# The first attention layer of a 16x112x512 decoder: from 128-wide masked scores to 32x32 diagonal blocks turned by VectorE, with one set of layer-norm statistics

## What is computed

```python
def _L0_attn_ref(x, weight_qkv, weight_proj):      # 16 heads of 32, 4 key/value heads
    seq, batch, hidden = x.shape                   # 16, 112, 512: attention runs over the 16
    qkv = (x.reshape(-1, hidden) @ weight_qkv.T).reshape(-1, 4, 192)
    q, k, v = ...                                  # 4 query heads share one key and value head
    scores = jnp.einsum('bhqd,bhkd->bhqk', q, k) * scale
    scores = jnp.where(causal, scores, -inf)       # 16 x 16 for each of the 112 columns of x
    attn = jnp.einsum('bhqk,bhkd->bqhd', softmax(scores), v)
    return attn @ weight_proj.T

x = x + _L0_attn_ref(_layernorm(x), ...)
x = x + _L0_xattn_ref(_layernorm(x), ctx_2048, ...)   # begins with a second layer norm,
                                                      # then divides by 4 scales and rounds to fp8
```

## Time and profile before

| | us |
|---|---|
| median of 3 runs (lowest, highest) | 3667.01 (3666.86, 3668.47) |
| profiled execution | 3677.25 |
| its span, first to last instruction | 3675.5 |
| first layer: first instruction of the loop stage / first maxima of tile 0 / first maxima of tile 13 / last rounding | 26.7 / 40.1 / 291.3 / 342.6 |
| busy in the span | PE 92%, weight loads 73%, DVE 68%, ACT 47%, POOL 26% |

### The profile page before, as it was taken

The page is one execution under the profiler, slowest core; times in us unless marked ns, Lnnn a source line. Parts: engine busy times, 40 slices in busy tenths (PEclk is TensorE's granted clock), DMA queues, the critical chain, the costliest instruction groups (busy, mean ns, idle before and its releaser), DMA issues. The chain is left out here.

```text
span 3675.5 us, 54660 instructions
## 1 busy us (share of the span) xinstructions
PE 3372.4 (92%) x17976; PEld 2700.6 (73%) x17976; DVE 2494.2 (68%) x6490; ACT 1715.9 (47%) x4059; POOL 952.2 (26%) x999
## 2 busy tenths in 40 slices
PE   6884999998799999989999996999989979998999
PEld 4552787787578778777878774888868757776887
DVE  4888889888466666756666666699856555558333
ACT  4653445444343433443443432688627655441222
POOL 2654344444222222332222222200133310000000
PEclk9886999999999999999999997999999989999999
DMA  6113001001100000110000005899930034433000
GB/s 221 21 20 79 0 0 46 23 0 56 44 28 20 19 28 20 55 59 23 20 28 19 20 9 187 290 410 400 353 88 2 12 126 122 124 105 104 11 10 21
DMA packets 113697, 296.12 MB, mean 81 GB/s; under 512 B 38032, under 2 KB 42128, under 8 KB 107776
## 3 DMA queue, kind: packets, MB, share of 16 engines
q1 hardware_dynamic: 107376, 276.39, 21.3%
q0 software_dynamic: 6160, 17.67, 1.6%
HBM read 251.65 MB, written 41.68 MB: 80 GB/s over the span
## 5 line engine op out<-in xcount | busy, mean ns | idle before, releaser
L40 PE MATMUL bank<-w,cross_ctx_part 128*125 128x512 f32 x1536 | 517.2, 418 | 8.1 <-DVE cross_qn L1090 4.7
L40 PEld LDWEIGHTS bank<-w,cross_ctx_part 128*125 128x125 f32 x1536 | 281.8, 187 | 93.5 <-DVE cross_kn L1090 14.5
L1000 ACT ACTIVATE cross_prob<-bank,cross_neg_max 112x375 f32<-112x375 f32 x256 | 147.0, 574 | 359.0 <-DVE cross_neg_max L1096 359.0
L40 PE MATMUL bank<-w_low,cross_ctx_part 128*125 128x512 f32 x768 | 303.7, 395 | 0.0
L1096 DVE TENSOR_REDUCE cross_neg_max<-bank 112x1 f32<-112x375 f32 x256 | 134.0, 524 | 198.0 <-PE bank L872 195.4
L40 PE MATMUL bank<-moe_wt,moe_zT 128*128 128x448 f32 x1176 | 265.1, 374 | 2.1 <-DVE moe_zT L1726 1.5
L1716 DVE TENSOR_TENSOR moe_wt<-moe_raw,moe_wt 128x1792 fp32r<-128x1792 f32 (+1 forms) x111 | 231.6, 2107 | 17.2 <-ACT moe_wt L1614 15.6
L40 PE MATMUL bank<-w,self_xq 128*112 128x512 f32 x512 | 213.7, 417 | 24.1 <-DVE w_low L595 24.0
L40 PEld LDWEIGHTS bank<-moe_wt,moe_zT 128*128 128x128 f32 x1176 | 216.1, 190 | 17.8 <-issue 1.7
L40 PE MATMUL bank<-mlp_zT,mlp_signs 128*128 128x448 f32 x1024 | 220.7, 368 | 5.7 <-DVE mlp_zT L2406 5.7
L772 POOL TENSOR_TENSOR cross_ve<-cross_mv,eps 125x4 f32<-125x4 f32 (+1 forms) x160 | 31.9, 200 | 730.7 <-DVE cross_mv L1081 730.7
(11 more groups left out here) (406 smaller groups left out, 8523.5 us busy)
## 6 DMA issues: line engine op xcount, KB each, us to landing
moe_raw<-in_moe_w SPq DMA_DIRECT2D x74, 896.0 KB, 7.7
moe_raw<-in_moe_w SPq DMA_DIRECT2D x37, 1024.0 KB, 8.2
stream<-in_L1f SPq DMA_DIRECT2D x32, 768.0 KB, 4.2
cross_ctx_raw<-in_ctxT SPq DMA_DIRECT2D x32, 750.0 KB, 4.1
wide_ctxT<-in_ctxT SPq DMA_DIRECT2D x16, 750.0 KB, 4.2
wide_ctx_rows<-in_ctx SPq DMA_DIRECT2D x16, 750.0 KB
expert_rows<-a_zeros SPq DMA_DIRECT2D x1, 8960.0 KB, 26.9
moe_zrow<-expert_rows SPq DMA_DIRECT2D x35, 256.0 KB, 7.8
```

The source lines that it names most:

```text
L40: mm = pe.matmul(out, a, b, start=first and n == 0, stop=last and n == len(pairs) - 1)
L1000: op = act.activation(prob[:, t % SLOTS, i, :], score_bank(t)[0:S, i * NK:(i + 1) * NK], ACT.Exp, bias=neg_max[:, h:h + 1], accum_out=tota ...
```

## The change

- The rows of a tile are ordered by position first (i, b) instead of (b, i), so the 16 rows of a position are neighbours and two positions fill a strip of 32 rows. The host lays `x` out so; the store to `x1` and the copy in `take_z2T` turn the order back.
- `scores` computes only the four 32x32 diagonal blocks of each head. The keys are the stationary operand, so the scores arrive with keys on partitions; strip j of key head r sits in bank r, partitions 32j to 32j+31, with 4 heads x 32 queries as columns. The mask matmuls have 128 columns instead of 512.
- `tops` turns all 128x512 scores out of the four banks with one VectorE transpose of 32x32 blocks (`STREAM_TRANSPOSE`), and takes all 16 maxima per row with one reduction. The exponentials are 32 wide and work in place. `turn_probs` does one reciprocal, one division on DVE (POOL's `divide` is gone) and a second VectorE transpose; `transpose_probs` and `take_probsT` are gone.
- `weigh_values(t)` is now 16 matmuls of 32x32 by 128 columns into banks 0 to 3 and stands one cycle later, after `project_out(t - 1)`; `project_out(t)` stands two cycles after its scores, `transpose_z2(t)` three.
- The statistics of the second norm are derived from those of the first: one `measure`, one power, one `normalise_twice`.
- DVE runs a cycle more: `shift` (with the clipping) and `round_back` of tile t - 4 in cycle t. The mask takes two selections.

The core of the diff; lines that it takes away from the functions printed above are left out where the new ones replace them:

```diff
-        self.ps = [ctx.enter_context(nc.psum_tensor(f"bank{i}", [P, 512], F32)) for i in range(8)]
+        self.banks = ctx.enter_context(nc.psum_tensor("bank", [P, 8, 512], F32))
+        self.ps = [self.banks[:, i, :] for i in range(8)]
...
                                pattern=[[-1, P]], channel_multiplier=1).then_inc(s["masked"], 1)
...
+            pool.affine_select(out=mask[:], in_=mask[:], compare_op=ALU.is_ge, fill=MASKED, base=0,
+                               pattern=[[1, P]], channel_multiplier=-1).then_inc(s["masked"], 1)
+            pool.wait_ge(s["masked"], 2)
+            pool.affine_select(out=mask[:], in_=mask[:], compare_op=ALU.is_ge, fill=MASKED, base=0,
+                               pattern=[[-B, P // B], [0, B]], channel_multiplier=1).then_inc(s["masked"], 1)
...
+            for j in range(4):
+                near = slice(NEAR * j, NEAR * j + NEAR)
+                dve.tensor_copy(mask4[near].rearrange("p (c t) -> p c t", t=NEAR),
+                                mask[near, None, near].to_broadcast([NEAR, 4, NEAR]))
...
+            def root(t):
+                pool.wait_ge(s["vareps"], t + 1)
+                pool.tensor_tensor(rstd[:, t:t + 1], ve[:, t:t + 1], k.half[:, 0:1], ALU.pow).then_inc(s["rooted"], 1)
+            root(0)
+            for t in range(1, NT):
+                root(t)
+                scale_rows(t - 1)
             scale_rows(NT - 1)
...
             def scores(t):
                 pe.wait_ge(s["q_ready"], t + 1)
                 pe.wait_ge(s["k_ready"], t + 1)
...
+                wait(pe, s["out_low"], t - 1)
                 for r in range(4):
...
+                    pe.matmul(ps[r][:, 0:4 * NEAR], ident16[:], mask4[:], start=True, stop=False)
+                for j in range(4):
                     for r in range(4):
...
+                        mm = pe.matmul(ps[r][strip(j), 0:4 * NEAR].rearrange("p (c t) -> p c t", t=NEAR),
+                                       kT[strip(r), strip(j)], qT[strip(r), :, strip(j)], start=False, stop=True)
                 mm.then_inc(s["scores_in_psum"], 1)
             def project_out(t):
                 pe.wait_ge(s["out_low"], t + 1)
+                wait(pe, s["x_done"], t)
                 for c in range(DC):
...
             def weigh_values(t):
...
+                pe.wait_ge(s["probsT_ready"], t + 1)
+                pe.wait_ge(s["scores_turned"], min(t + 2, NT))
+                wait(pe, s["out_low"], t)
                 for r in range(4):
...
+                    for j in range(4):
+                        mm = pe.matmul(ps[j][strip(r), 0:4 * NEAR], kv[strip(j), t % 3, P + 32 * r:P + 32 * r + 32],
+                                       probT[strip(j), t % 2, r].rearrange("p c t -> p (c t)"), start=True, stop=True)
                 mm.then_inc(s["outT_in_psum"], 1)
...
+            for t in range(NT + 3):
+                if t < NT:
+                    scores(t)
                 if t + 1 < NT:
                     project_qkv(t + 1)
+                if 2 <= t < NT + 2:
+                    project_out(t - 2)
+                if 1 <= t < NT + 1:
+                    weigh_values(t - 1)
+                if t + 1 < NT:
                     transpose_q(t + 1)
...
                     transpose_k(t + 1)
...
+                if t >= 3:
+                    transpose_z2(t - 3)
                 if t + 2 < NT:
                     transpose_z(t + 2)
...
+            def exponentials(t):
+                act.wait_ge(s["minus_max"], t + 1)
+                for r in range(4):
+                    for c in range(4):
+                        op = act.activation(prob[:, r, c, :], prob[:, r, c, :], ACT.Exp,
+                                            bias=neg_max[:, r, c:c + 1], accum_out=total[:, r, c:c + 1])
                 op.then_inc(s["exp_done"], 1)
...
+                    op = act.activation(z2T[:, c, :].rearrange("p (b i) -> p b i", b=B),
+                                        tiled(6)[:, c, :].rearrange("p (i b) -> p b i", b=B), ACT.Identity,
+                                        scale=ln_cols[:, c:c + 1], bias=ln_cols[:, DC + c:DC + c + 1])
...
+            for t in range(NT + 3):
+                if t < NT:
+                    exponentials(t)
                 if t + 1 < NT:
                     take_q(t + 1)
...
                     take_kv(t + 1)
...
+                if 1 <= t < NT + 1:
+                    out_high(t - 1)
                 if t + 1 < NT:
                     take_qT(t + 1)
...
                     take_kT(t + 1)
...
+                if t >= 3:
+                    take_z2T(t - 3)
                 if t + 2 < NT:
                     z_high(t + 2)
...
+                if t >= NT:
+                    weights.round_high(act, 0, (QS, KS, VS)[t - NT])
...
             def tops(t):
                 dve.wait_ge(s["scores_in_psum"], t + 1)
...
+                wait(dve, s["probsT_ready"], t)
+                dve.transpose(prob[:].rearrange("p r c t -> p r (c t)"), near_scores).then_inc(s["scores_turned"], 1)
+                dve.wait_ge(s["scores_turned"], t + 1)
+                dve.tensor_reduce(neg_max[:], prob[:], AX.X, ALU.max, negate=True).then_inc(s["minus_max"], 1)
+            def turn_probs(t):
+                dve.wait_ge(s["exp_done"], t + 1)
+                dve.reciprocal(inverse[:], total[:]).then_inc(s["inverse_ready"], 1)
+                dve.wait_ge(s["inverse_ready"], t + 1)
+                dve.tensor_tensor(prob[:], prob[:], inverse[:, :, :, None].to_broadcast([T, 4, 4, NEAR]), ALU.mult)\
+                    .then_inc(s["divided"], 1)
+                dve.wait_ge(s["divided"], t + 1)
+                wait(dve, s["outT_in_psum"], t - 1)
+                dve.transpose(probT[:, t % 2].rearrange("p r c t -> p (r c t)"), prob[:].rearrange("p r c t -> p (r c t)"))\
+                    .then_inc(s["probsT_ready"], 1)
             def out_low(t):
                 dve.wait_ge(s["out_high"], t + 1)
...
+                dve.tensor_tensor(in_strips(oT[1]), heads_of_strips(), in_strips(oT[0]).bitcast(F32), ALU.subtract)\
+                    .then_inc(s["out_low"], 1)
...
+            def measure(t):
                 dve.wait_ge(s["x_done"], t + 1)
...
+                dve.bn_stats(stats[:], xt[:, t, :]).then_inc(s["stat"], 1)
+                dve.wait_ge(s["stat"], t + 1)
+                dve.bn_aggr(mv[:, t, :], stats[:]).then_inc(s["centre"], 1)
+                dve.wait_ge(s["centre"], t + 1)
+                dve.tensor_scalar(ve[:, t:t + 1], mv[:, t, 1:2], 1.0 + EPS, EPS * EPS, ALU.mult, ALU.add)\
+                    .then_inc(s["vareps"], 1)
+            def normalise_twice(t):
+                dve.wait_ge(s["rooted"], t + 1)
                 if t == 0:
                     dve.wait_ge(s["cleared"], 16)
                 wait(dve, s["z2T_in_psum"], t)
...
+                dve.tensor_scalar(z2[:], xt[:, t, :], mv[:, t, 0:1], rstd[:, t:t + 1], ALU.subtract, ALU.mult)\
                     .then_inc(s["z2_ready"], 1)
...
+            def shift(t):
                 dve.wait_ge(s["scaled"], t + 1)
...
+            for t in range(NT + 4):
+                if t < NT:
+                    tops(t)
+                if t >= 4:
+                    shift(t - 4)
+                if 3 <= t < NT + 3:
+                    normalise_twice(t - 3)
                 if t + 2 < NT:
                     normalise(t + 2)
...
+                if t < NT:
+                    turn_probs(t)
+                if 2 <= t < NT + 2:
+                    add_out(t - 2)
+                if 1 <= t < NT + 1:
+                    out_low(t - 1)
+                if 2 <= t < NT + 2:
+                    measure(t - 2)
+                if t >= 4:
+                    round_back(t - 4)
                 if t + 2 < NT:
                     z_low(t + 2)
...
-    lay["x_by_position"] = a["x"].reshape(16, 14, 8, 512).transpose(1, 0, 2, 3).reshape(1792, 512)
+    lay["x_by_position"] = a["x"].reshape(16, 14, 8, 512).transpose(1, 2, 0, 3).reshape(1792, 512)
```

More of the change, by code:

```diff
@@ L2507, in _ @@
         def _(pool):
-            pool.memset(mask[:], MASKED).then_inc(s["made"], 1)
+            pool.memset(mask[:], 0.0).then_inc(s["made"], 1)
             pool.memset(zeros[:], 0.0).then_inc(s["made"], 1)
@@ L2571, in first_layer @@
              "qT_in_psum", "kT_in_psum", "q_ready", "k_ready", "scores_in_psum", "minus_max", "exp_done",
-             "inverse_ready", "probs_ready", "probsT_in_psum", "probsT_ready", "outT_in_psum", "out_high",
-             "out_low", "y_in_psum", "x_done", "cleared", "stat1", "centre1", "vareps1", "rooted1", "z1_ready",
-             "stat2", "centre2", "vareps2", "rooted2", "z2_ready", "z2T_in_psum", "z2T_taken", "scaled", "clipped",
-             "exponent", "magic", "shifted", "rounded")
+             "scores_turned", "inverse_ready", "divided", "probsT_ready", "outT_in_psum", "out_high",
+             "out_low", "y_in_psum", "x_done", "cleared", "stat", "centre", "vareps", "rooted",
```

(17 more changed lines are left out.)

190 lines of the change are left out of this document (25 added, 165 removed).

## The result

| | before | changed |
|---|---|---|
| median of the runs (lowest, highest), us | 3667.74 (3666.86, 3671.02) | 3632.43 (3630.29, 3634.33) |
| profiled execution / its span | 3677.25 / 3675.5 | 3634.33 / 3632.6 |
| first maxima of tile 0 / of tile 13 / end of the last rounding | 40.1 / 291.3 / 342.6 | 37.5 / 249.8 / 308.9 |
| mean cycle, tile 5 to 13 | 20.22 | 18.75 |
| first read of `xq` by the second layer | 343.8 | 310.1 |

The ratio is 0.9902, 95% interval 0.9885 to 0.9919: 35.3 us faster by the medians, against a forecast of 25.4. The loop stage gives 33.7 of it. The two profiled executions differ by 42.9 us; the other 9 lie in the expert layer (1063.4 us before, 1054.4 after, from its first turned tile to the last layer's), which the change doesn't touch.

A forecast was written before the change was run, and what follows sets the result against it. A chain through four engines bounds the loop, with PE waiting for POOL's divisions. Stage terms 38.6 + 62.8 + 136.5 + 18.9 + 16.1 + 44.3 = 317.2 against 342.6 us: 25.4 less, so 3667.0 - 25.4 = 3641.6 us; range 3605 to 3656.

The forecast's parts named there:

- The cycle of 13.95 us: DVE's queue in one full cycle: its instructions sum to 13.95 us if nothing holds it.
- The stop: POOL's scaling enters between two roundings of `round_back`, and DVE stands 3.5 us per cycle, making it 17.5 us.
- The half clock: PE idles 4.9 us for `z_low`, then runs at half clock: 2.0 us lost per cycle, making it 19.5 us.
- the rival at full clock: PE keeps full clock after its wait: cycle 17.5 us, eight cycles by 2.0, 3626 us; chance 0.13.
- Scores and values at 1.2 us each: PE's sixteen 32x32 products of 128 columns cost 1.2 us each for scores and values, priced by today's scores.
- 3634: Time in us if scores and values cost 0.4 us each, values 0.8 us earlier on PE's path in ten cycles.
- The turn: DVE's 32x32 transpose of 512 columns, two added per tile, taken at 0.65 us each.
- The tail: Last cycles, all DVE and POOL: 13.2, 12.6 and 18.5 us, together 44.3 us.
- Slower: PE's 32x32 products don't overlap across strips: sixteen cost 8.4 us, cycle 27.0, 3747 us; chance 0.05.
- The scaling that misses the roundings: POOL's scaling falls beside `z_low` and the maxima instead of `round_back`: cycle 15.6 us at full clock, 3607 us; chance 0.15.
- The dear turn: DVE's 32x32 transpose costs 2.3 us: 1.3 us more in eight cycles, about 2.5 in four, 3662 us; chance 0.06.
- What stood behind the old cycle: Before, DVE's `shift` held up POOL's third and fourth divisions (4.03 us); PE stood 3.12 us and resumed at half clock.

The follow-up runs named there:

- experiment 11: Roundings behind the second normalisation in every cycle, against the kernel with scaling ahead of the power and reordered tail; cycle 14.15 us, next layer at 266.0 us.
- experiment 12: Kernel with scaling ahead of the power and roundings behind the second normalisation in every cycle, timed against before: 3608.08 us, ratio 0.9793.
- experiment 5: Changed kernel with 20 small identity products on PE ahead of its wait for `z_low`, from the sixth cycle on; cycle 16.78 us, next layer at 295.5 us.
- experiment 2: Changed kernel with `round_back` directly behind `shift`; cycle 15.85 us, next layer at 292.2 us.
- experiment 3: Changed kernel with `round_back` directly behind `shift` and POOL's scaling ahead of the power; cycle 14.46 us, next layer at 280.0 us.
- experiment 4: Changed kernel with POOL's scaling in four instructions instead of one; cycle 16.04 us, next layer at 290.5 us.
- experiment 7: Kernel before, with `shift` moved behind `add_out` and the statistics of the rows; cycle 17.51 us, next layer at 319.1 us.

## Where the prediction was right and wrong

**The direction, the size and the mechanism held; one price on the path did not.** The forecast of 3641.6 us was 9.2 too high. The measured 3632.4 lies inside the stated range, but at the very edge of the 3632 to 3655 of the forecast's own case. Of the 8.3 us that the stage gained beyond 25.4, 1.1 lie in the opening (first maxima 37.5, not 38.6), 0.5 in the first five cycles (62.3 against 62.8), 5.4 in the cycles from tile 5 to 13 (150.0 against 155.4), 1.3 in the tail.

- **The cycle of 13.95 us, if nothing holds DVE.** Durations of neighbours overlap by some hundredths in each row; the cycles without any wait, one in experiment 11 and two in experiment 12, took 13.5. In the changed kernel only a part of this error counts, since DVE waits at `add_out` and `out_low` in each full cycle and what is short ahead of them is waited out there. From the start of `out_low` to the next tile's turn the sum has 8.3 us and the rows 8.04: about 2 of the 5.4 us.
- **The stop.** Forecast 3.5 us in each cycle, measured 3.41. That the scaling would fall into `round_back`, and that which rounding it hits does not matter, held: the fourth in the cycle shown, one of the first three in that of experiment 5. The Trainium skill (SBUF — State Buffer, Who interferes with whom) says that a VectorE instruction with two SBUF inputs contends with a GpSimd instruction that reads SBUF, and that their shared ports are an exclusive lock. The rows agree: nothing is lost beside the turn out of the banks and the reduction (0.72 and 0.69 us, experiment 2) and the statistics (0.68, experiment 3), and 0.84 us beside a quarter (experiment 4). One SBUF input alone does not make an instruction safe, as the forecast took it to be. In the kernel before, `normalise`, which writes SBUF from SBUF, takes 1.58 us instead of 0.54 in each of the nine cycles in which the scaling runs beside it (here until 153.76):

```profile
152.47 1.58 DVE L2846 TENSOR_SCALAR a_z<-x,mean_var,rstd 128x512 f32<-128x512 f32 x1
```

- **The half clock.** Forecast 2.0 us lost per cycle, measured 2.0 (18.75 - 16.78). Of the rival at full clock, priced at 16 us, experiment 5 gives 14.6.
- **Scores and values at 1.2 us each, the term that failed.** They take 0.50. I had priced them by products that span all four column groups. The Trainium skill (TensorE: Matmul & The Clock Gate, Measured speedup vs the span model) has the figures from which I had worked out an estimate of 0.4, and that was nearer. For the scores the error was free: `z_low` ends PE's wait, which grew from 4.9 to 5.9. The values are on the path of each full cycle, because DVE waits 0.52 us more behind `add_out` for what ACT takes of them. ACT begins 0.69 us after the values' start (165.21), not 1.2:

```profile
165.90 0.60 ACT L2781 ACTIVATE a_oT<-bank 128x512 fp32r<-128x512 f32 x1 [2.94 <-PE bank L2714]
```

That is 0.5 us in each of eight cycles, about 4 of the 5.4 us; some 0.7 us went back elsewhere. So 3634, the time that the forecast worked out from this estimate, lay nearest to the measured one, and mostly for its own reason, though it counted 0.8 us in ten cycles. The rest of its nearness is luck.
- **The turn** at 0.70 to 0.71 instead of 0.65, **the exponentials** 0.306 apart instead of 0.27: both still hidden or small. The normalisations stay at 0.55.
- **The tail** held to 1.3 us: its roundings read 5.30 for three in cycles 14 to 16, as the earlier trace rows.
- **The rivals.** Slower, by products that don't overlap: refuted by the 0.50 us. The scaling that misses the roundings: not here, but made on purpose in experiment 2, where the cycle was 15.85 for the rival's 15.6. The dear turn: refuted.
- **What stood behind the old cycle.** The reading that `shift` holds up the divisions was right, its weight too low: in experiment 7 moving it takes nearly 3 us off each cycle.

That the 32x32 blocks themselves pay is shown only in the better order: both kernels freed of their stop read 17.51 and 14.15 to 14.46 us per cycle. What part of that belongs to the blocks and what to the single statistics in a cycle that DVE bounds wasn't tried. Nor was what the half clock still costs the fastest kernel: its clock over 99 to 235 us is 0.88 (experiment 11), and no filling products ran there.

## What to carry to other kernels

Before taking work out of a cycle, ask what stands still in it and why: here an instruction of GpSimd stopped VectorE for nearly its whole length, TensorE waited behind that and lost its clock, and moving one call by a few lines in the old kernel was worth three quarters of what rewriting the attention brought. Lay GpSimd's long instructions beside VectorE's reads of PSUM, reductions and statistics (not beside a rounding with two SBUF inputs, nor, by the rows of `normalise`, beside a `tensor_scalar` from SBUF to SBUF), or cut them so that VectorE gets in between; put what releases TensorE ahead of what can stop. A move that shortens the full cycles can lengthen the tail, where nothing covers the chain, so read both ends of the loop.

## What the hardware showed that was not expected

- A 128x2048 product on GpSimd costs 3.61 us in one piece and, in four, 4.04 where nothing holds them and 5.03 where a rounding gets in, and the four stop VectorE for 0.84 to 1.7 us instead of 3.41.
- 20 idle products of 128 columns (4.73 us of PE's time) go with a clock of 1.00 instead of 0.81 and are worth 14.6 us although their results are thrown away.
- A layer that no edit touches moved by up to 24 us from chip to chip and between executions, near the size of the effect studied. Its first 481 us keep the DMA engines 83% busy in the changed kernel; what bounds it wasn't tested. A landmark ahead of it, repeated to 0.1, 0.7 and 1.2 us in three kernels that were profiled twice, decided what the totals couldn't.
